# A transformer layer on eight cores: the next block's LayerNorm moved ahead of the first FFN product, two more buffer pairs, and a wider spacing of the first LayerNorm

## The reference

```python
x = L0_attn_x                                   # (32, 2048, 1024), f32
x = x + attn(layernorm(x))                      # 16 heads of 64, causal, latent projections, q and k RMS-normed
x = x + ffn(layernorm(x))                       # gelu(h @ w1 + b1) @ w2 + b2, w1 1024 x 4096, w2 4096 x 1024
```

## Time and profile before

| | us |
|---|---|
| median of 2 runs | 11080.3 |
| lowest and highest | 11079.92, 11080.68 |
| the profiled execution | 11067.92 |
| its span, slowest core (core 7) | 11066.4 |
| span of the core that was quickest (core 5) | 11025.5 |

### The profile page before, as it was taken

How to read it: one execution, slowest core, us unless ns; L and a number is a source line. 1 busy time by engine, 2 the same in 40 slices (tenths; PEclk the granted TensorE clock), 3 DMA queues, 4 the chain that set the end, 5 groups by cost and what they waited for, 6 DMA issues and landing times.

```text
span 11066.4 us, 103769 instructions; the slowest of 8 cores (11025.5 to 11066.4 us)
## 1 busy us (share of the span) xinstructions
PE 5954.4 (54%) x29865; PEld 2744.7 (25%) x29865; DVE 4851.7 (44%) x16593; ACT 2676.5 (24%) x4512; POOL 158.9 (1%) x312
## 2 busy tenths in 40 slices
PE   3344545534454554344546533445454677778878
PEld 1122222212222222112222221122221333333333
DVE  4555545555555554555545545555553111111111
ACT  2222222222222322222222222222221211222111
POOL 0000000000000000000000000000000000000000
PEclk5555555555555555555555555555555899889989
DMA  0000000000000000000000000000002211111110
GB/s 18 20 3 18 2 18 2 19 3 18 20 1 19 1 2 18 20 2 18 2 18 1 2 18 20 3 18 2 16 1 55 47 39 29 31 38 39 37 33 31
DMA packets 63864, 192.32 MB, mean 17 GB/s; under 512 B 8808, under 2 KB 8848, under 8 KB 62288
## 3 DMA queue, kind: packets, MB, share of 16 engines
q0 software_dynamic: 42624, 117.46, 4.7%
q1 hardware_dynamic: 20688, 68.24, 1.9%
HBM read 168.89 MB, written 67.11 MB: 21 GB/s over the span
## 4 chain that ended last, share of the span: by engine, by line
PE 41%; DVE 35%; issue 13%; ACT 8%; DVEq 1%; another core or an unknown queue 1%; ACTq 0%; SPq 0%; DMA 0%; POOL 0%; POOLq 0%
DVE S_sb L731 8%; DVE PT L817 7%; PE ps_c L833 7%; PE pt_x L807 5%; PE pt_y L807 5%; PE ps_a L1066 4%; PE ps_c L1042 4%; PE ps_b L1066 4%; PE ps_d L1042 4%; DVE mcol L748 2%; DVE qn_tok L586 2%; DVE kst L612 2%; ACT P_B L778 2%; DVE S_sb L741 2%; DVE qst L515 2%
## 5 line engine op out<-in xcount | busy, mean ns | idle before, releaser
L778 ACT ACTIVATE P_A<-S_sb,negm,rstdq_win 128x256 bf16<-128x256 f32 (+15 forms) x512 | 662.4, 1294 | 3667.4 <-PE pt_y L807 2560.4
L833 PE MATMUL ps_c<-PT,vst 128*64 128x512 bf16 (+3 forms) x2560 | 734.3, 556 | 1181.0 <-DVE PT L817 1181.0
L718 PE MATMUL ps_s<-kst,qst 128*128 128x512 bf16 (+3 forms) x1280 | 656.3, 530 | 522.8 <-DVE S_sb L731 391.1
L817 DVE COPY PT<-pt_x 128x1024 bf16<-128x1024 bf16 (+1 forms) x640 | 408.1, 638 | 1026.6 <-PE pt_x L807 1026.5
L817 DVE COPY PT<-pt_y 128x1024 bf16<-128x1024 bf16 (+2 forms) x640 | 374.0, 584 | 1089.8 <-PE pt_y L807 1089.8
L731 DVE TENSOR_SCALAR_CACHE_REDUCE S_sb<-ps_s 128x512 f32<-128x512 f32 (+2 forms) x1152 | 673.5, 614 | 309.5 <-PE ps_s L718 292.9
L778 ACT ACTIVATE P_B<-S_sb,negm,rstdq_win 128x256 bf16<-128x256 f32 (+15 forms) x512 | 662.0, 1293 | 511.1 <-DVE negm L761 511.0
L807 PE MATMUL pt_x<-id_bf,P_A 128*128 128x128 bf16 x2304 | 358.5, 305 | 745.5 <-ACT P_B L778 745.5
L600 PE MATMUL pt_y<-id_bf,qn_tok 128*64 128x128 bf16 x1024 | 132.1, 310 | 883.5 <-DVE qn_tok L586 883.5
L833 PEld LDWEIGHTS ps_c<-PT,vst 128*64 128x64 bf16 x2560 | 204.3, 127 | 1484.6 <-issue 1484.6
L1042 PE MATMUL ps_c<-Xn2T,w1b 128*128 128x512 bf16 x2048 | 502.6, 390 | 8.7 <-ACT hT L1052 7.6
(11 more groups left out here) (190 smaller groups left out, 8440.0 us busy)
## 6 DMA issues: line engine op xcount, KB each, us to landing
x_buf<-x SPq DMA_DIRECT2D x64, 512.0 KB, 7.2
x2s<-x_buf POOLq DMA_DIRECT2D x64, 512.0 KB, 6.3
x_buf<-x2s SPq DMA_DIRECT2D x64, 512.0 KB, 8.7
y<-x_buf POOLq DMA_DIRECT2D x64, 512.0 KB, 4.1
xln<-x POOLq DMA_DIRECT2D x64, 256.0 KB, 4.0
xln<-x2s POOLq DMA_DIRECT2D x64, 256.0 KB, 3.6
w1b<-W POOLq DMA_DIRECT2D x8, 1024.0 KB, 41.7
w2b<-W POOLq DMA_DIRECT2D x32, 256.0 KB, 77.2
```

The source lines that it names most:

```text
L718: P.step("pe", lambda t, h=h, qt=qt, off=off, w=w, ps=ps: t.matmul(ps[:, 0:w], qstack[h][:, qt * 128:(qt + 1) * 128], kstack[h][:, off:off ...
L778: P.step("ac", lambda a, P_sb=P_sb, po0=po0, klen=klen, slot=slot, spar=spar, rc=rc: a.activation(out=P_sb[:, po0:po0 + klen], in_=S2[spar ...
L817: P.step("dv", lambda v, par=par, qt_min=qt_min: v.tensor_copy(PT2[par][:].rearrange("p (h f) -> p h f", f=512) [:, :, qt_min * 128:512], ...
L833: P.step("pe", lambda t, hi=hi, grp=grp, v0=v0, par=par, qt_min=qt_min, j=j, nj=nj: t.matmul(ps_c[hi * HD:(hi + 1) * HD, qt_min * 128:512] ...
```

## The change

It has four parts.

- In the attention half `xn_bf` becomes a pair of buffers, `xn_bf2[tc % 2]`, each with its own `Rel`.
- The pieces of `w1q` are taken off in every third slot instead of every second.
- In the FFN half `Xn2T` becomes a pair, `Xn2T2[s % 2]`, with `r_Xn2Tb[s % 2]`. `xn2`, `pt_x`, `musum` and the rest stay single.
- `emit_ln2(s + 1)` is written ahead of step 1 of block s instead of between steps 2 and 4.

```diff
-        xn_bf = sb("xn_bf", [128, D], BF16)
+        xn_bf2 = [sb(f"xn_bf{i}", [128, D], BF16) for i in range(2)]
...
+        r_xnbf2 = [Rel(), Rel()]
...
-                            out=xn_bf[:], in_=xln[par][:], func=AF.Square,
+                            out=xn_bf2[tc % 2][:], in_=xln[par][:], func=AF.Square,
                             accum_out=sqsum[:]),
-                            wait=[(d_xl[par], ld), dv_ln] + r_xnbf.waits(),
+                            wait=[(d_xl[par], ld), dv_ln]
+                            + r_xnbf2[tc % 2].waits(),
...
-                        r_xnbf.set(pe_ln)
+                        r_xnbf2[tc % 2].set(pe_ln)
...
-                                if w1q and slot_ctr[0] % 2 == 0:
+                                if w1q and slot_ctr[0] % 3 == 0:
                                     w1q.pop(0)()
...
-            Xn2T = fsb("Xn2T", [128, NFC * 512])
+            Xn2T2 = [fsb(f"Xn2T{i}", [128, NFC * 512]) for i in range(2)]
+            r_Xn2Tb = [Rel(), Rel()]
...
-                        wait=[pe_ft] + (r_Xn2T.waits() if tc == 0 else []),
+                        wait=[pe_ft]
+                        + (r_Xn2Tb[s_ % 2].waits() if tc == 0 else []),
...
                 if s not in ln2_marks:
                     emit_ln2(s)
+                if s + 1 < B * NB:
+                    emit_ln2(s + 1)
                 xn2T_ready = ln2_marks[s]
...
-                            Xn2T[:, fc * 512:(fc + 1) * 512],
+                            Xn2T2[s % 2][:, fc * 512:(fc + 1) * 512],
...
-                r_Xn2T.set(pe_f)
-                if s + 1 < B * NB:
-                    emit_ln2(s + 1)
+                r_Xn2Tb[s % 2].set(pe_f)
                 pp2 = [(ps_a, r_psa), (ps_b, r_psb)]
```

More of the change, by code:

```diff
@@ L421, in chain @@
                             wait=[ac_ln, f_xl[0], f_xl[1]], inc=ac_ln)
-                        P.step("dv", lambda v, par=par: v.tensor_scalar(
-                            out=xn_bf[:], in0=xln[par][:], scalar1=negmu[:],
+                        P.step("dv", lambda v, par=par, tc=tc: v.tensor_scalar(
+                            out=xn_bf2[tc % 2][:], in0=xln[par][:],
+                            scalar1=negmu[:],
                             scalar2=rstd[:], op0=ALU.add, op1=ALU.mult),
-                            wait=[ac_ln] + r_xnbf.waits(), inc=f_xl[par])
+                            wait=[ac_ln] + r_xnbf2[tc % 2].waits(),
+                            inc=f_xl[par])
                     return chain
@@ L434, in tr @@
                                 pt_x[:, fc * 128:(fc + 1) * 128],
-                                xn_bf[:, fc * 128:(fc + 1) * 128], id_bf[:]),
+                                xn_bf2[tc % 2][:, fc * 128:(fc + 1) * 128],
+                                id_bf[:]),
                                 wait=([(f_xl[par], xn_done), (po_set, POSET)]
@@ L1012, in emit_ln2 @@
                     r_xn2.set(pe_ft)
-                    P.step("dv", lambda v, tc=tc: v.tensor_copy(
-                        Xn2T[:].rearrange("p (c f) -> p c f", f=512)
+                    P.step("dv", lambda v, tc=tc, s_=s_: v.tensor_copy(
+                        Xn2T2[s_ % 2][:].rearrange("p (c f) -> p c f", f=512)
                         [:, :, tc * 128:(tc + 1) * 128],
                         pt_x[:].rearrange("p (c f) -> p c f", f=128)),
-                        wait=[pe_ft] + (r_Xn2T.waits() if tc == 0 else []),
+                        wait=[pe_ft]
+                        + (r_Xn2Tb[s_ % 2].waits() if tc == 0 else []),
                         inc=dv_f)
@@ L1041, in build_program @@
                     for fc in range(NFC):
-                        P.step("pe", lambda t, fc=fc, hc=hc, ps=ps: t.matmul(
+                        P.step("pe", lambda t, fc=fc, hc=hc, ps=ps, s=s: t.matmul(
                             ps[:, :],
```

## The result

The changed kernel takes 11322.5 us in the median of 11 runs; the kernel before takes 11077.1 in 10 runs beside them. That is 245.4 us more. The ratio of the mean times is 1.0246, with a 95% interval of 1.0207 to 1.0285: slower. (In some runs a whole die runs at a lower clock; the ratios leave them out, the medians do not.) The forecast was 11343, within 11300 to 11385.

The account below looks back on a forecast made before the run. TensorE bounds the FFN half, so its pauses are paid in full. Terms -393 + 645 + 25 + 5 = +282 us, less 19 of clock, give +263 on the median 11080.3: 11343 us, range 11300 to 11385.

Parts of the forecast that it names:

- the spacing: Attention half, LayerNorm 1 pieces in every third slot: +5 us over 15 windows, bounds -10 and +15.
- gaps between products, 15: FFN blocks: TensorE's pause between first and second product vanishes, 26.2 us at each of 15, -393 us.
- boundaries, 14: Between FFN blocks: TensorE waits for adds, stores, loads and LayerNorm, 46.1 us more at each of 14, +645 us.
- LayerNorm 1 ahead of block 0: Start of the FFN half: block 0's first product starts at 8667.3 instead of 8642.11, 25.2 us on.
- The bound and the two places: FFN half: TensorE's idle time between products is paid in full; gap inside a block about 26.2 us, none at boundaries.
- The second buffers: Second Xn2T makes the move legal but moves nothing; second xn_bf gains nothing, at most 5.4 us.
- The clock under load: TensorE's granted clock late in the run: longer pauses give about half of 38.8 us back, 19 us.
- A: Block boundary: shorter load waits plus full clock back put the time between the bounds but within 2%; chance 0.09.
- B: FFN products without rest for 122 us lose more clock, time above 11385 us; chance 0.08.
- C: Block boundary: TensorE passes the waiting transposes, so the first product overlaps the LayerNorm, 10717 us; chance 0.01.
- D: Attention half: wider spacing hides 60 us of the pieces, time within 2%; chance 0.03, of faster 0.01.
- The signs to look for: No gap between products, boundary pause 45 to 48 us, block 0 about 25 us later, 30 table loads, shifted reciprocal distances.

Follow-up runs that it names:

- the last two runs: Kernel before with LayerNorm 1 pieces in slots 43, 46, ... 64 (last reciprocal 8430.6 to 8437.0 us), or in every second, odd slot (8422.3 to 8427.8 us).
- the move alone: Kernel before with only emit_ln2(s+1) ahead of the first product and the pair of Xn2T: 11299.6 us, ratio 1.0224.
- the two cut pauses: Changed kernel with xln loads not waiting for the stores, 11186.5 us; or with loads of tiles 0 and 1 ahead of the stores, 11026.9 and 11027.0 us.
- the split: Changed kernel with the LayerNorm's transposes behind the first product, its chains still ahead (four xn2 buffers, one Xn2T): 11235.8 us.
- the odd slots: Kernel before with LayerNorm 1 pieces in every second slot, odd ones (43, ... 55), none at a seam: cores at 10998.8 to 11003.0 us.
- the last one: Changed kernel with LayerNorm woven into the second product, pieces in odd slots, y transposes behind the next chunk's matmuls: 10599.0 us, ratio 0.9594.

## Why the prediction was right, and where it was not

The median moved by 245 us against a forecast of 263, and the largest error is one term with the wrong sign, the spacing (23 us). The ledger compares the slowest cores, core 7 before and core 4 after, in us:

| term | forecast | measured | from |
|---|---|---|---|
| gaps between products, 15 | -393 | -393 | 26.4 to 0.2 between the last and first matmul |
| boundaries, 14 | +645 | +644 | pause 47.6 instead of 1.6, mean of 14 |
| LayerNorm 1 ahead of block 0 | +25.2 | +25.2 | first product at 8649.6, 7.5 later, and the landmark 17.7 earlier |
| spacing | +5 | -17.7 | landmark 8452.4 to 8434.7 |
| clock, and what is left | -19 | -13 | all 32 products together, 2003 to 1990 |
| sum | +263 | +245 | spans |

**The bound and the two places** were right. The pause of 46.1 us beyond the old 1.6 was worked out from three rows of a trace in which it did not exist, and it came to 46.0 on the core that sets the time. That it met it within 0.1 us is luck: over the eight cores the added pause lies between 43.3 and 46.0, because the load wait differs by core (15.8 to 18.4 us a boundary before, 15.5 to 17.8 after), and the forecast was read from one of the cores where it is long. The mid gap vanished as block 15 had shown. One slow start of the clock per block before, one after: the first product after a pause takes 57.1 us instead of 55.8, the second 64.8 instead of 66.3 on cores at full clock, so nothing.

**The second buffers** were right: no gain from `xn_bf`, by its own run. The 3 us that it costs there were not foreseen.

**Every third slot** was wrong in sign: +5 with -10 and +15 as bounds, measured -17.7. The step that failed is the split of the distances of the earlier trace rows. It took 6 us for a chain at a seam from the distance of the pairs 3 to 4 alone and 6.9 for one inside, by giving each `tr` 1.35 us of VectorE's time, so that a swap from seam to inside cost 0.9 us a window. The bound of -10 came from no row. The same view of the changed kernel, core 4, window 3:

```profile
1818.23 0.19 DVE L797 RECIPROCAL rl_buf<-l_buf 128x8 f32<-128x8 f32 x1
...
1894.41 0.20 DVE L797 RECIPROCAL rl_buf<-l_buf 128x8 f32<-128x8 f32 x1 [1.53 <-ACT P_B L783]
...
1972.35 0.19 DVE L797 RECIPROCAL rl_buf<-l_buf 128x8 f32<-128x8 f32 x1
...
2051.56 0.19 DVE L797 RECIPROCAL rl_buf<-l_buf 128x8 f32<-128x8 f32 x1
...
2127.64 0.20 DVE L797 RECIPROCAL rl_buf<-l_buf 128x8 f32<-128x8 f32 x1 [2.38 <-ACT P_B L783]
```

From pair 3 to 7 it is 309.4 us, before 310.9: 1.5 less where I had 0.9 more. The brackets say what I passed over: before, two of the middle reciprocals wait 1.53 us for the last exponential, which queues behind the chain on ScalarE; here only one does. Those brackets stood in the earlier trace rows, and I averaged over them. The runs showed in its place a gain of 1.2 us a window (17.7 over 15). The wait at the seam is part of it at most: by the last two runs the rest, and the reason, stay open.

**The clock under load** was a guess at half of 38.8 us back. In this execution core 4 spent 204 us at 0.81, as long as core 7 did before, and the products together got 13 us shorter. Four of these come on cores at full clock too. The other nine are not explained: nearly all of the time at 0.81 lies inside products in both profiles (202 of 205 us before, all 204 after). The size was near by luck; the reasoning (more rest, more clock) is not shown. The runs scatter too much: no core fell to 0.81 in the profiles of the move alone, of the two cut pauses, of the split and of the odd slots, but the odd slots have no more rest in the FFN half than the kernel before, which spent 205 us at it.
**The range.** That the median fell inside 11300 to 11385 was in part luck. The 11 runs lie between 11271.0 and 11447.3 us, and only four of them lie inside the range; two are below it and five above. A range for one run would have had to be twice as wide.

**Rivals.** A (within 2%) did not come: the boundary was shorter on quick cores, 44.9 to 47.6 us by core, but the slowest core sets the time. B (over 11385) did not come in the median, but five of the 11 runs, 11391.5 to 11447.3, lie there, with less granted clock on four of the eight cores than on the others. C is excluded by two runs: neither TensorE nor ScalarE lets anything pass. The two runs are the changed kernel, in which TensorE stands behind its transposes, and the one with the transposes behind the product. D was right in direction, with 18 of the 60 us it needed.

**The signs to look for.** I expected 30 table loads and there are 29 (15 for Gelu, 14 for Ln): block 15 follows with no LayerNorm in between, so its Gelu needs no load. At 1.28 us each, the table loads that are gone are under 3 us of the whole. The pause of 45 to 48 us and the missing gap came. Block 0's first product starts 7.5 us later and not 25, since the attention half ends 17.7 us earlier. In window 3 the distance from pair 6 to 7 grew (69.4 to 76.1 us) and the one from 4 to 5 shrank (85.6 to 77.9), as said, but the one from 5 to 6 did not grow (79.8 to 79.2) and the total was not the same.

## What to carry to other kernels

Before moving a piece of work earlier, write down for every engine what stands behind it in its queue afterwards, and follow each of its inputs back to what triggers it: here the loads hung on the stores of the block before, and a hidden wait of 18 us came to stand ahead of the first product of 14 blocks. The second `Xn2T` made the move legal; whether it gained was decided by the in-order queues. Weave such a piece, in slices, into the stage in which the engine that it needs is idle (ScalarE in the second product), and put each slice's consumer a slice later.

## What the runs showed of the hardware

- In these profiles the granted clock of 0.81 comes on two neighbouring cores together (2 and 3, 4 and 5, or 6 and 7), on other pairs in other runs and on none in five of the 12, for 121 to 479 us of an FFN half of some 2000 to 2700 us, while the other cores spend at most 10 us at it in the whole run. It makes the slowest core later by 30 to 105 us over four runs of one kernel (the last one). A change of less than half a per cent is therefore read from single cores, not from the median.
- Two 256 KB casting loads issued right behind 2 MB of stores, instead of after their landing, brought the data 5.9 us earlier in the mean over the cores, where the wait taken out was 5.7: the stores in flight did not slow them measurably.
